# A mixture of experts behind differential attention: rows by number, results in token order

## The chip, the cores and the metric
One NeuronCore of a Trainium2 chip runs the kernel. The metric is the device time of one execution in microseconds, lower is better. The kernel before took 1133.09 us in the median of 3 runs (1131.99 to 1135.56).

## The reference
Input `x` is 4 x 1024 x 256, so 4096 tokens of 256 values, float32. With `xn = layernorm(x)` it computes:

```
q, k  = xn wq^T, xn wk^T          # 8 heads x 2 halves x 32
v     = xn wv^T                   # 8 heads x 32
a     = softmax(q1 k1^T / sqrt(32), causal) - lambda * softmax(q2 k2^T / sqrt(32), causal)
s     = rmsnorm(a v, in groups of 4 values) * (1 - L_INIT), times wo^T
top 2 of 8 experts per token by xn router^T + bias, weights = softmax of the two logits
f_e   = ((clip(up, 7) + 1) * g * sigmoid(1.702 g)) down_e + bias_e,   g = min(gate, 7)
out   = x + s * silu(w0 * f_e0(xn) + w1 * f_e1(xn))
```

Each expert has a 256 x 512 matrix (gate and up) and a 256 x 256 matrix (down).

## The kernel before
It has four blocks that run one after another. At the end of each all engines meet before the next begins.

**Block 1, layer norm, projections, routing.** A loop over 8 chunks of 512 tokens. VectorE normalises, TensorE turns the rows and multiplies by the weights, with each operand split into a high and a low part. ScalarE (`high_parts`) and VectorE (`low_parts`) move the products to four `PARTS` buffers, which SyncE stores to DRAM (L306 to L313); ScalarE waits for the store before it uses a buffer again. Per chunk SyncE also stores 1152 KB of zeros to `xs_dram` (L303), so that places that no token fills are defined, and stores the normalised rows to `xn_dram`. VectorE ranks the experts of each token (`rank`). After the last chunk it turns the choices into slots (L488 to L539). Each expert gets whole tiles of 128 slots, 72 tiles in all. A token's slot is the first slot of its expert plus the number of tokens before it. For that VectorE makes prefix sums over 32 token tiles (five doublings, L497 and L498) and adds the rank inside the tile (L528 to L534).

**Block 2, attention.** 16 iterations of two heads, each of 8 frames (`p` 0 to 7) that pair a long and a short query tile. TensorE scores and turns probabilities, VectorE takes maxima and combines the two softmaxes, ScalarE exponentiates and copies out. GpSimd copies V (`copy_v`, L795), moves each frame's output from `Ob` to `VO` (`keep_rows`, L808), and keeps the sums (`keep_d1`, L833). It also sorts the tokens: per iteration it loads two tiles of `xn_dram` (L814), copies their slots (L815), and issues four indirect DMAs (L826), each of which scatters 128 rows of 1 KB to their slots in `xs_dram`. SyncE loads Q and K one iteration ahead, and an expert's weights and biases in each of the iterations 0 to 7.

**Block 3, experts.** 72 tiles, two sets of buffers (`u` 0 and 1), in 36 loop iterations. SyncE loads a tile of `xs_dram` as soon as TensorE has turned the one two tiles earlier (`xs_turned`, L1166). TensorE works in the order gate and up of tile n+1, turning tile n+2, down of tile n-1, turning the activation of tile n. VectorE runs `activate` (n), `hidden` and `gate` (n+1), `output` (n-1, L1381). ScalarE stores the output from its own queue (`store`, L1312) to `ys_dram`, in slot order. GpSimd does nothing here.

**Block 4, join.** 8 chunks of 512 tokens. GpSimd copies the chunk's slots and weights (L1482, L1483) to fixed tiles and gathers each token's two result rows from `ys_dram`:

```
pool.wait_ge(picked, credited(b, 4, 2 * h + 1))
pool.sem_inc(gather_begun, 1)
for i in range(CT):
    for k in range(TOP_K):
        pool.indirect_dma_start(yg[h][:, i, k, :], None, ys_dram, ...yslot[h][:, i, k:k + 1]...)
```

That is 8 indirect DMAs per chunk. ScalarE scales the first expert's rows (L1562), VectorE adds the second's (L1635), normalises the attention output (L1622 to L1654), and gates and adds (L1660 to L1670). TensorE turns and projects in between. SyncE loads `x` and stores the result.

Of the kernel before, what the change touches and what calls it, by code (L numbers as in the profile page):

```python
# [6 lines left out]
F32 = mybir.dt.float32  # L7
# [60 lines left out]
LONG0, SHORT, LONG1 = 0, 1, 2  # L68
UNITS = 3 * NP
# [31 lines left out]
SORT_AT = {1: (0, 0), 2: (0, 1), 3: (1, 0), 4: (1, 1)}  # L101
# [10 lines left out]
def build(nc, x, wqk, wv, wo, lam, rw, rb, gu, gub, dn, dnb, out):  # L112
    with ExitStack() as ctx:
# [11 lines left out]
        xs_dram = nc.dram_tensor("xs_dram", (SLOT_TILES * P, D), F32, kind="Internal").ap()  # L125
        ys_dram = nc.dram_tensor("ys_dram", (SLOT_TILES * P, D), F32, kind="Internal").ap()
# [19 lines left out]
        slot_of = sb("slot_of", [P, T // P, TOP_K], U32)  # L146

# [16 lines left out]

        consts_done = sem("consts_done")
# [5 lines left out]
        with ExitStack() as ph:  # L171
# [3 lines left out]
            zeros = sb("zeros", [P, SLOT_TILES // NCH * D], where=ph)  # L175
            before = sb("before", [P, E, E], where=ph)
# [3 lines left out]
            count_f = sb("count_f", [P, SLOT_TILES], where=ph)  # L180
            count_128 = sb("count_128", [P, T // P], where=ph)
            logits = sb("logits", [P, T // P, E], where=ph)
            cmp = sb("cmp", [P, T // P * E * TOP_K + 2 * SLOT_TILES * E], where=ph)
            ranks = sb("ranks", [P, 3, QT, E], where=ph)
            chosen = sb("chosen", [P, TOP_K, T // P, E], where=ph)
            chosen_b = sb("chosen_b", [P, T // P, E], BF16, where=ph)
            top = sb("top", [P, 6, T // P], where=ph)
            run = [sb(f"run{i}", [P, T // P, E], where=ph) for i in range(2)]
            per_e = sb("per_e", [P, 8, E], where=ph)
# [36 lines left out]
            zeros_ready = sem("zeros_ready")  # L226
            zeros_stored = sem("zeros_stored")
# [14 lines left out]
            with nc.Block() as block:  # L242
                @block.gpsimd
                def _(pool):
# [19 lines left out]
                    nc.gpsimd.memset(zeros[:], 0.0).then_inc(zeros_ready, 1)  # L264

                    nc.gpsimd.memset(before[:], 1.0).then_inc(const_step, 1)
# [5 lines left out]
                    nc.gpsimd.affine_select(out=before[:], in_=before[:], compare_op=ALU.is_gt, fill=0.0, base=0,  # L272
# [6 lines left out]
                    nc.gpsimd.tensor_copy(count_f[:], count_i[:]).then_inc(const_step, 1)  # L279
                    pool.wait_ge(const_step, 16)  # L280
                    nc.gpsimd.tensor_scalar(count_128[:], count_f[:, 0:T // P], float(P), None, ALU.mult
# [3 lines left out]
                def _(sp):  # L285
# [13 lines left out]
                    sp.wait_ge(zeros_ready, 1)  # L299
                    xs_v = xs_dram.rearrange("(n p r) d -> n p (r d)", p=P, r=SLOT_TILES // NCH)  # L300
# [30 lines left out]
                    sp.wait_ge(zeros_stored, 16 * NCH)  # L331

                @block.vector
                def _(dve):
# [58 lines left out]
                    def rank(b):  # L393
# [16 lines left out]
                        then(nc.vector.tensor_tensor(c3, c3, before[:].rearrange("p e f -> p (e f)").unsqueeze(1)  # L410
# [65 lines left out]

                    steps = [0]
# [7 lines left out]
                    NT = T // P  # L485
                    ck = cmp[:, 0:TOP_K * NT * E].rearrange("p (k t e) -> p k t e", k=TOP_K, e=E)

                    nc.vector.tensor_tensor(top[:, 2], top[:, 1], top[:, 0], ALU.subtract).then_inc(gap_ready, 1)  # L488

                    dve.wait_ge(ranks_bank, 1)  # L490
                    pre = bank6[:, 0:NT * E].rearrange("p (t e) -> p t e", e=E)
                    tot = bank7[:, 0:NT * E].rearrange("p (t e) -> p t e", e=E)
                    nc.vector.memset(run[0][:, 0:1, :], 0.0)
                    then(nc.vector.tensor_copy(run[0][:, 1:NT, :], tot[:, 0:NT - 1, :]))
                    src, span = 0, 1
                    while span < NT:
                        nc.vector.tensor_copy(run[1 - src][:, 0:span, :], run[src][:, 0:span, :])  # L497
# [1210 lines left out]
```

## Time and profile before

| | |
|---|---|
| median of 3 runs | 1133.09 us |
| profiled execution | 1132.22 us |
| its span | 1130.4 us |
| TensorE, VectorE, ScalarE, GpSimd busy | 83%, 83%, 69%, 20% |
| DMA | 178.11 MB, 158 GB/s |
| granted clock of TensorE | 0.945 |

The span is from the first to the last instruction. Busy time counts instructions of an engine, without those that only wait, branch or issue DMAs on SyncE and ScalarE. GpSimd is different: its indirect DMAs are made by the engine itself and count as busy. "Idle before" names what ended an engine's wait. The four blocks lie at about 0 to 182, 182 to 760, 769 to 1013 and 1013.6 to 1130 us.

### The profile page before, as it was taken

What the parts mean: (1) busy time and instruction counts of PE and PEld (TensorE: products, weight loads), DVE (VectorE), ACT (ScalarE), POOL (GpSimd) and SP (SyncE); (2) the same over time, 40 slices, a digit from 0 to 9 for tenths busy, and PEclk for the clock granted to TensorE, in tenths of its full rate; (3) what the DMA queues carried; (4) which work ended last, traced back from release to release, by engine and by line L of the source; (5) the groups of instructions that cost most, each with busy time, mean ns of one, the idle gap of its engine ahead of it and who ended that gap; (6) DMA issues with size and microseconds to landing.
All of it is one profiled execution on the core that took longest, in us unless ns stands there. A gap on an engine that the chain in (4) does not pass through costs nothing. (4 is left out here: it accounts for less than half of the span.)

```text
span 1130.4 us, 25744 instructions
## 1 busy us (share of the span) xinstructions
PE 941.0 (83%) x6626; PEld 657.1 (58%) x6627; DVE 937.8 (83%) x1872; ACT 777.8 (69%) x1982; POOL 225.3 (20%) x427
## 2 busy tenths in 40 slices
PE   5888875989889898998989989876999999962665
PEld 4666653666666666666666666653555555541544
DVE  6676757999999999999999999963777777764887
ACT  3444334999999999999999999972333333325563
POOL 2000000122223222232222322220000000007771
PEclk9999985999999999999999999997999999996677
DMA  7988967578676786766657566501222222223553
GB/s 274 353 318 304 329 256 202 126 179 197 165 178 154 178 194 164 178 156 138 152 120 165 129 140 151 118 20 50 80 79 83 83 80 79 84 82 104 163 179 118
DMA packets 92410, 178.11 MB, mean 158 GB/s; under 512 B 11744, under 2 KB 50144, under 8 KB 91360
## 3 DMA queue, kind: packets, MB, share of 16 engines
q1 hardware_dynamic: 74336, 147.38, 48.6%
q0 software_dynamic: 7680, 20.98, 6.3%
q10 hardware_dynamic: 10368, 9.44, 2.5%
q8 instruction: 11, 0.18, 0.1%
q14 instruction: 15, 0.12, 0.0%
HBM read 108.56 MB, written 69.21 MB: 157 GB/s over the span
## 5 line engine op out<-in xcount | busy, mean ns | idle before, releaser
L1032 DVE TENSOR_REDUCE nmax<-bank 128x1 f32<-128x1024 f32 (+3 forms) x256 | 259.9, 1015 | 4.2 <-PE bank L864 4.1
L965 ACT ACTIVATE Pr_long<-bank,nmax 128x1024 f32<-128x1024 f32 (+3 forms) x256 | 252.2, 985 | 10.9 <-DVE nmax L1032 10.8
L992 ACT COPY AT<-bank 128x512 f32<-128x512 f32 (+3 forms) x384 | 177.2, 494 | 3.8 <-PE bank L903 1.8
L862 PE MATMUL bank<-Ks_first,Qs_first 128*128 128x512 f32 (+3 forms) x384 | 124.2, 413 | 31.0 <-ACT Pr_short L979 19.8
L979 ACT ACTIVATE Pr_short<-bank,nmax 128x128 f32<-128x128 f32 (+3 forms) x256 | 138.4, 541 | 8.9 <-DVE nmax L1050 1.5
L1224 PE MATMUL bank<-gu_sb,xsT 128*128 x288 | 140.1, 610 | 4.7 <-DVE hid L1341 0.5
L903 PE MATMUL bank<-ident,Pr_long 128*128 128x128 f32 x832 | 127.4, 280 | 18.0 <-DVE Pr_long L1082 17.9
L1082 DVE SCALAR_TENSOR_TENSOR Pr_long<-Pr_long,coef 128x1024 f32<-128x1024 f32 (+3 forms) x128 | 137.4, 1074 | 0.0
L862 PE MATMUL bank<-Ks_second,Qs_second 128*128 128x512 f32 (+3 forms) x384 | 119.5, 400 | 19.8 <-ACT Pr_short L979 19.5
L864 PE MATMUL bank<-maskb,identb 128*128 128x128 bf16 x512 | 118.2, 233 | 0.0
L926 PE MATMUL bank<-AT,Vj 128*32 128x128 f32 x2304 | 108.7, 278 | 0.0
L903 PEld LDWEIGHTS bank<-ident,Pr_long 128*128 128x128 f32 x832 | 90.4, 142 | 31.4 <-issue 27.0
L808 POOL COPY VO<-Ob 128x64 f32 (+1 forms) x128 | 30.3, 237 | 386.3 <-ACT Ob L1001 386.0
L645 PE MATMUL bank<-XNT_parts,wqk_parts 128*128 128x512 f32 x384 | 95.1, 406 | 9.7 <-DVE PARTS L432 8.2
L862 PEld LDWEIGHTS bank<-Ks_first,Qs_first 128*128 128x128 f32 x384 | 66.4, 202 | 59.2 <-ACT Pr_short L979 39.3
L862 PEld LDWEIGHTS bank<-Ks_second,Qs_second 128*128 128x128 f32 x384 | 63.5, 193 | 48.6 <-ACT Pr_short L979 40.5
L645 PEld LDWEIGHTS bank<-XNT_parts,wqk_parts 128*128 128x128 f32 x384 | 73.9, 194 | 28.2 <-DVE PARTS L432 9.3
L864 PEld LDWEIGHTS bank<-maskb,identb 128*128 128x128 bf16 x512 | 49.9, 97 | 67.8 <-issue 50.6
L581 ACT ACTIVATE PARTS<-bank 128x512 fp32r<-128x512 f32 x64 | 38.3, 598 | 60.9 <-PE bank L645 30.8
L1050 DVE TENSOR_REDUCE nmax<-bank 128x1 f32<-128x512 f32 (+1 forms) x128 | 79.0, 618 | 1.3 <-PE bank L864 0.7
L926 PEld LDWEIGHTS bank<-AT,Vj 128*32 128x32 f32 x2304 | 74.4, 109 | 8.8 <-issue 0.3
L1250 PE MATMUL bank<-dn_sb,act_T 128*128 x288 | 76.1, 387 | 2.8 <-ACT act_T L1303 2.7
(147 smaller groups left out, 1633.4 us busy)
## 6 DMA issues: line engine op xcount, KB each, us to landing
q_parts<-PARTS SPq DMA_DIRECT2D x32, 512.0 KB, 3.7
k_parts<-PARTS SPq DMA_DIRECT2D x32, 512.0 KB, 3.7
Qs_first<-q_parts SPq DMA_DIRECT2D x64, 256.0 KB
Ks_first<-k_parts SPq DMA_DIRECT2D x64, 256.0 KB
Qs_second<-q_parts SPq DMA_DIRECT2D x64, 256.0 KB, 5.8
Ks_second<-k_parts SPq DMA_DIRECT2D x64, 256.0 KB, 6.8
xs_dram<-zeros SPq DMA_DIRECT2D x8, 1152.0 KB, 7.3
xs<-xs_dram SPq DMA_DIRECT2D x72, 128.0 KB, 2.0
```

Source lines behind the costliest of these rows:

```text
L645: last = nc.tensor.matmul(qkbank[i % 4], wqk_parts[:, w, c, i * P:(i + 1) * P], XNT_parts[:, r, c, :], start=((c, w, r) == products[0]), s ...
L862: nc.tensor.matmul(at[:, c0:c1], Qs[head][:, m, q * P:(q + 1) * P], Ks[head][:, m, c0:c1], start=True, stop=(c1 < N))
L864: return nc.tensor.matmul(at[:, N - P:N], identb[:], maskb[:], start=False, stop=True)
L903: last = nc.tensor.transpose(tb[u % BANKS][:, i * P:(i + 1) * P], probs[:, 0, kb * P:(kb + 1) * P], ident[:])
L926: last = nc.tensor.matmul(ob[DH * g:DH * (g + 1), 0:P], Vj[head][:, kb, :], AT[unit(p, k) % 6][:, i * P:(i + 1) * P], start=first, stop=final,
L965: nc.scalar.activation(long_probs(p)[:, m, 0:N], long_slot[m][:, 0:N], ACT.Exp, bias=nmax[:, 4 * p + m:4 * p + m + 1], scale=1.0, accum_ou ...
L979: nc.scalar.activation(short_probs(p)[:, m, 0:N], short_at(p, m)[:, 0:N], ACT.Exp, bias=nmax[:, 4 * p + 2 + m:4 * p + 3 + m], scale=1.0, a ...
L992: nc.scalar.copy(AT[u % 6][:, 0:w], tb[u % BANKS][:, 0:w]).then_inc(unit_out, 1)
L1032: nc.vector.tensor_reduce(nmax[:, 4 * p + m:4 * p + m + 1], long_slot[m][:, 0:N], AX.X, ALU.max, negate=True).then_inc(long_maxed, 1)
L1050: nc.vector.tensor_reduce(nmax[:, 4 * p + 2 + m:4 * p + 3 + m], short_slot[:, 0:N], AX.X, ALU.max, negate=True).then_inc(short_maxed, 1)
L1082: nc.vector.scalar_tensor_tensor(out=probs[:, 0, 0:N], in0=probs[:, 1, 0:N], scalar=coef[:, 2 * p + 1:2 * p + 2], in1=probs[:, 0, 0:N], op ...
L1224: last = nc.tensor.matmul(hbank[u], xsT[u][:, c, :], gu_sb[:, c, bass.ds(e, 1), :].rearrange("p o n -> p (o n)"), start=(c == 0), stop=(c ...
```

## The change
- **Row numbers, not rows, are sorted.** In block 1 SyncE stores a 36 KB table of default numbers to `ids_dram` once; the stores of zeros go. In attention, iterations 1 to 8, GpSimd scatters one 4-byte number for each token and choice (`k * 4096 + token`) to its slot in `ids_dram`: 8 indirect DMAs per iteration, 64 in all. The row loads (L814) and the scatters of rows go. After iteration 9's loads SyncE reads the whole table back as 128 x 72 words (`slot_rows`). In the last iteration GpSimd works out the token of each slot (`slot_tokens`) and gathers the first tile of rows.
- **Block 3.** GpSimd gathers each tile of rows from `xn_dram` (`rows_in`), and scatters each tile of results to `y_dram` in token order (`results_out`). SyncE's loads and ScalarE's stores go. VectorE's `output` waits for `rows_ready`, which GpSimd signals after it has copied the tile's row numbers.
- **Block 4.** The eight gathers per chunk go; SyncE loads the chunk's two result rows per token with two plain DMAs of 512 KB.
- **Prefix sums** and slot numbers move from VectorE at the end of block 1 to GpSimd in iteration 0 of attention, frames 0 to 4. Their tiles lie in the memory of the biases of experts 2 to 7, whose loads wait for `routed`.
- **All four blocks** are made with `no_gpsimd_drain=True`.

```diff
-                        sp.dma_start(xs_v[b * 2 + h], zeros[:]).then_inc(zeros_stored, 16)
+                    sp.dma_start(ids_dram.rearrange("(q n) o -> q (n o)", n=2 * P), no_rows[:]).then_inc(ids_cleared, 16)
...
+                    nc.vector.tensor_copy(pre, bank6[:, 0:NT * E].rearrange("p (t e) -> p t e", e=E))
+                    nc.vector.tensor_copy(tot, bank7[:, 0:NT * E].rearrange("p (t e) -> p t e", e=E))
...
+                    then(nc.vector.tensor_reduce(tokens, bank7[:, 0:NT * E].rearrange("p (t e) -> p e t", e=E), AX.X,
+                                                 ALU.add))
...
+                    sp.wait_ge(routed, ROUTE_OPS)
...
+                    sp.wait_ge(ids_sorted, 16 * SORT_ITS * NP)
+                    with nc.allow_non_contiguous_dma("one word of each slot"):
+                        sp.dma_start(slot_rows[:], ids_dram.rearrange("(n p) o -> p (n o)", p=P)
+                                     ).then_inc(rows_known, 16)
...
+                    def double(src, span):
+                        nc.gpsimd.tensor_copy(run[1 - src][:, 0:span, :], run[src][:, 0:span, :])
+                        then(nc.gpsimd.tensor_tensor(run[1 - src][:, span:, :], run[src][:, span:, :],
+                                                     run[src][:, 0:NT - span, :], ALU.add))
...
+                        for n in SORT_AT.get(p, ()):
+                            i, k = n // TOP_K, n % TOP_K
+                            pool.indirect_dma_start(ids_dram, bass.IndirectOffsetOnAxis(sort_slot[:, i, k:k + 1], 0),
+                                                    sort_id[:, i, k:k + 1], None).then_inc(ids_sorted, 16)
...
+            with nc.Block(no_gpsimd_drain=True) as block:
+                @block.gpsimd
+                def _(pool):
+                    def rows_in(it, u):
+
+                        pool.wait_ge(xs_turned, seen(it, u - 2))
+                        nc.gpsimd.tensor_copy(xs_token[u][:], slot_tokens[:, bass.ds(2 * it + u, 1)]
+                                              ).then_inc(tokens_ready, 1)
+                        pool.wait_ge(tokens_ready, 2 * (it - 1) + u + 1)
+
+                        pool.sem_inc(gather_begun, 1)
+                        pool.indirect_dma_start(xs[u][:], None, xn_dram, bass.IndirectOffsetOnAxis(xs_token[u][:], 0)
+                                                ).then_inc(xs_loaded[u], 16)
+
+                    def results_out(it, u):
+
+                        if not (isinstance(it, int) and it == 0):
+                            pool.wait_ge(y_stored[u], 16 * it)
+                        nc.gpsimd.tensor_copy(ys_row[u][:], slot_rows[:, bass.ds(2 * it + u, 1)]
+                                              ).then_inc(rows_ready, 1)
+                        pool.wait_ge(rows_ready, 2 * it + u + 1)
+                        pool.wait_ge(y_ready, seen(it, u))
+
+                        pool.sem_inc(gather_begun, 1)
+                        pool.indirect_dma_start(y_dram, bass.IndirectOffsetOnAxis(ys_row[u][:], 0), ys[u][:], None
+                                                ).then_inc(y_stored[u], 16)
...
+                    with pool.Fori(1, NIT3 - 2) as it:
                         for u in range(2):
-                            load(it, u)
+                            rows_in(it + 2, u)
+                            results_out(it, u)
...
-                    nc.vector.wait_ge(y_stored[u], 16 * (it + 1))
+
+                    nc.vector.wait_ge(rows_ready, 2 * it + u + 1)
...
+                    def load_y(b, h):
+                        for k in range(TOP_K):
+                            sp.dma_start(yg[h][:, :, k, :], y_v[k, b, h]).then_inc(y_loaded[h], 16)
```

## Rows read from the trace of the kernel before
**Rows 1.** Busy time by stage: start:end, length, engines (x instructions), clock, DMA share, GB/s
```profile
0.00:182.00 182.00, 134.95 (x578) 106.16 (x579) 120.78 (x344) 73.06 (x141) 6.69 (x27) 0.95 0.86 303
...
182.00:760.40 578.40, 516.53 (x4992) 368.97 (x4992) 559.71 (x960) 558.28 (x1537) 148.15 (x320) 0.98 0.66 151
...
771.00:1012.00 241.00, 231.38 (x864) 137.00 (x864) 173.93 (x432) 83.46 (x216) 0.00 (x0) 0.99 0.24 77
...
1013.60:1130.40 116.80, 58.18 (x192) 44.97 (x192) 83.41 (x136) 63.00 (x88) 70.41 (x80) 0.69 0.46 144
```
**Rows 2.** The chain that ended last, its shares of the span by line, from the page
```profile
POOL yg L1489 5%; DMA yg<-ys_dram,yslot 0%; PE bank L1535 0%; POOL yslot L1482 0%; ACT ff L1562 0%; DVE root L1641 0%; POOLq L1447 0%; DVE ff L1635 0%; DVE ft L1666 0%; ACT L1571 0%; DVE xr L1670 0%; DVE ft L1660 0%; DVE On L1654 0%; POOL yw L1483 0%; ACT root L1571 0%
```
**Rows 3.** Timeline of the expert stage: start us, us, engine, line
```profile
883.08 0.42 DVE L1381 SCALAR_TENSOR_TENSOR ys<-bank,dnb_sb 128x256 f32<-128x256 f32 x1
...
889.56 0.42 DVE L1381 SCALAR_TENSOR_TENSOR ys<-bank,dnb_sb 128x256 f32<-128x256 f32 x1
...
890.15 0.34 ACTq L1312 DMA_DIRECT2D ys_dram<-ys  x1
```
**Rows 4.** Timeline of the last stage: first and last of VectorE's sums
```profile
1029.01 1.72 DVE L1635 SCALAR_TENSOR_TENSOR ff<-yg,yw,ff 128x256 f32<-128x256 f32 x4 [12.15 <-ACT ff L1562]
...
1112.06 1.67 DVE L1635 SCALAR_TENSOR_TENSOR ff<-yg,yw,ff 128x256 f32<-128x256 f32 x4 [1.16 <-ACT ff L1562]
```
**Rows 5.** The list of waits: us in total, times, longest
```profile
ACT ff L1562 <- DMA yg<-ys_dram,yslot: 30.3, 8, 12.2
```
**Rows 6.** Timeline of GpSimd in the last stage
```profile
1025.55 0.19 POOL L1483 COPY yw<-weight 128x8 f32 x1
...
1026.55 0.97 POOL L1489 DMA_INDIRECT yg<-ys_dram,yslot  x1 [0.81 <-POOL yw L1483]
...
1027.83 0.96 POOL L1489 DMA_INDIRECT yg<-ys_dram,yslot  x1 [0.30 <-issue]
```
**Rows 7.** Indirect DMAs by line: duration ns min/median/max, first and last start
```profile
L1489 POOL DMA_INDIRECT yg<-ys_dram,yslot x64: 949/957/1503, 1015.6 to 1107.5; - x64
...
L826 POOL DMA_INDIRECT xs_dram<-rows,row_slot x64: 983/1047/1238, 209.3 to 752.4; - x64
```
**Rows 8.** Timeline of GpSimd in attention
```profile
752.41 0.98 POOL L826 DMA_INDIRECT xs_dram<-rows,row_slot  x1 [0.45 <-issue]
```
**Rows 9.** Timeline at the ends of block 1 and of block 2
```profile
181.20 0.15 DVE L544 TENSOR_SCALAR lam_s<-lam_s 128x1 f32<-128x1 f32 x1
...
182.07 0.34 SPq L162 DMA_DIRECT2D Qs_second<-q_parts  x1
...
760.13 0.24 POOL L808 COPY VO<-Ob 128x64 f32<-128x64 f32 x1 [0.24 <-ACT Ob L1023]
...
768.86 3.30 SPq L1166 DMA_DIRECT2D xs<-xs_dram  x3
...
771.00 1.20 PE L1210 MATMUL bank<-ident,xs 128*128 128x128 f32 x4 [11.31 <-DMA xs<-xs_dram]
```
**Rows 10.** DMA issues: engine, count, KB each, median us to landing
```profile
xs_dram<-zeros SPq DMA_DIRECT2D x8, 1152.0 KB, 7.3
...
xr<-x SPq DMA_DIRECT2D x8, 512.0 KB, 3.5
...
xs_dram<-rows,row_slot POOLq DMA_INDIRECT x64, 3.6
...
yg<-ys_dram,yslot POOLq DMA_INDIRECT x64, 2.8
...
ys_dram<-ys ACTq DMA_DIRECT2D x72, 128.0 KB, 1.7
```
**Rows 11.** The list of waits, TensorE in block 1
```profile
PE bank L631 <- DVE XN L380: 20.4, 7, 10.2
```
**Rows 12.** Sum of busy time over the stretches 168:171 and 177.4:180.2
```profile
sum 5.80, PE 3.00 PEld 2.47 DVE 5.40 ACT 1.00 POOL 0.00; mean PE 1.50 PEld 1.24 DVE 2.70 ACT 0.50 POOL 0.00
```
**Rows 13.** VectorE's ratio in attention: duration ns min/median/max
```profile
L1069 DVE SCALAR_TENSOR_TENSOR coef<-dsum,lam_s,rec x128: 203/215/356, 188.9 to 753.1; 128x2 f32<-128x2 f32 x128
```

More of the change, by code:

```diff
@@ L68 @@
 LONG0, SHORT, LONG1 = 0, 1, 2
+ROUTE_OPS = 14
 UNITS = 3 * NP
@@ L493, in _ @@
[L493 to L497, printed above, removed]
-                        then(nc.vector.tensor_tensor(run[1 - src][:, span:, :], run[src][:, span:, :],
-                                                     run[src][:, 0:NT - span, :], ALU.add))
-                        src, span = 1 - src, 2 * span
+                    tokens, tiles, first, end, first_slot = (per_e[:, i] for i in range(5))
@@ L501, in _ @@
+                    then(nc.vector.tensor_reduce(tokens, bank7[:, 0:NT * E].rearrange("p (t e) -> p e t", e=E), AX.X,
+                                                 ALU.add))
                     low_parts(B - 1, 1, range(QKT // 2, QKT // 2 + 2))
-                    tokens, tiles, first, end, first_slot = (per_e[:, i] for i in range(5))
-                    then(nc.vector.tensor_tensor(tokens, run[src][:, NT - 1, :], tot[:, NT - 1, :], ALU.add))
-                    ce = cmp[:, 0:E * NT].rearrange("p (e t) -> p e t", e=E)
+                    ce = rcmp[:, 0:E * NT].rearrange("p (e t) -> p e t", e=E)
@@ L699, in build @@
             nmax = sb("nmax", [P, 2 * NQ], where=ph)
-            rows = [sb(f"rows{u}", [P, D], where=ph) for u in range(2)]
-            row_slot = [sb(f"row_slot{u}", [P, TOP_K], U32, where=ph) for u in range(2)]
+            sort_slot = sb("sort_slot", [P, NP // 2, TOP_K], U32, where=ph)
+            sort_id = sb("sort_id", [P, NP // 2, TOP_K], I32, where=ph)
             rec = sb("rec", [P, NQ], where=ph)
@@ L1120, in build @@
         with ExitStack() as ph:
-            xs = [sb(f"xs{u}", [P, D], where=ph) for u in range(2)]
+            xs = [xs_first, sb("xs_second", [P, D], where=ph)]
+            xs_token = [sb(f"xs_token{u}", [P, 1], I32, where=ph) for u in range(2)]
+            ys_row = [sb(f"ys_row{u}", [P, 1], I32, where=ph) for u in range(2)]
             xsT = [sb(f"xsT{u}", [P, HC, P], where=ph) for u in range(2)]
@@ L1129, in build @@
             ys = [sb(f"ys{u}", [P, D], where=ph) for u in range(2)]
-            xs_loaded = [sem(f"xs_loaded{u}") for u in range(2)]
+            tokens_ready = sem("tokens_ready")
+            rows_ready = sem("rows_ready")
+            gather_begun = sem("gather_begun")
             xs_turned = sem("xs_turned")
@@ L1404, in build @@
             yg = [sb(f"yg{h}", [P, CT, TOP_K, D], where=ph) for h in range(2)]
-            yslot = [sb(f"yslot{h}", [P, CT, TOP_K], U32, where=ph) for h in range(2)]
             yw = [sb(f"yw{h}", [P, CT, TOP_K], where=ph) for h in range(2)]
```

285 lines of the change are left out of this document (169 added, 116 removed).

## The prediction
> **What bounds the kernel now.** I read the totals by stage first, because the program has four blocks that follow one another. The first stage (0 to 182 us: layer norm, Q/K/V and router products) keeps the DMA engines 86% busy and TensorE 135 of 182 us. Attention (182 to 760) is VectorE's: 560 of 578 us. The expert stage (771 to 1012) is TensorE's: 231 of 241 us, with GpSimd at zero. The last stage (1014 to 1130) has GpSimd at 70 us, and the chain that ended last, read next, has GpSimd's gathers (L1489) as its longest line [rows 1, 2]. Then the distances inside the stages. Two outputs of one buffer, `ys`, lie 889.56 - 883.08 = 6.48 us apart, so an expert tile takes 3.24 us [rows 3]. The last stage's chunks go by GpSimd: the second halves of the expert sums (L1635) first start at 1029.01 and last at 1112.06, 83.05 / 7 = 11.86 us per chunk, and by the list of waits ScalarE waited 30.3 us for gathered rows [rows 4, 5]. The change takes transfers away from SyncE and ScalarE in the expert stage and gives them to GpSimd, so the price of one GpSimd transfer decides.
>
> **That price.** In the last stage the kernel already does what the new expert loop does: copy an index to a fixed place, wait for that copy, add to a semaphore, start the indirect DMA. The last copy before the DMA takes 0.19 us; from its end (1025.74) to the DMA's start (1026.55) are 0.81 us; the next DMA follows 0.30 after the end of the one before [rows 6]. The median gather is 0.957 us long on GpSimd, the median scatter 1.047 [rows 7]: I use 0.96 and 1.05. Where nothing waits for the copy's own completion, as in attention, the gap between copy and DMA is still 0.45 us [rows 8].
>
> **The expert stage, step by step.** For each of 72 tiles GpSimd now runs `rows_in` and `results_out`.
> - `rows_in`: copy 0.19, gap 0.81, gather 0.96: 1.96 us. Its wait on `xs_turned` is met in steady state, for TensorE has over a microsecond to spare by then.
> - `results_out`: copy 0.19. VectorE's output now waits for `rows_ready`, that is for this copy, and GpSimd then waits for that output: about 0.06 to reach VectorE (an estimate from the 0.17 us by which a store on ScalarE's queue follows an output, 889.98 to 890.15 [rows 3]), 0.42 for the output, 0.10 back; then 0.70 to the DMA's start (the 0.81 less 0.11 for the copy's own signal), and the scatter 1.05: 2.52 us.
> Together 4.48, taken as 4.45 us per tile. Behind GpSimd's wait for an output stand the next gather and its copy; behind VectorE's wait stand the next tile's activation and bias, 173.93 / 72 = 2.42 us of VectorE per tile with the output itself [rows 1], which fit into the rest. So GpSimd becomes the bound: 72 x (4.45 - 3.24) = +87.1 us. Below, without VectorE in the loop, 2 x (0.19 + 0.81) + 0.96 + 1.05 = 4.01, or +55. Above, with four hold-ups of 0.15 us by VectorE, 5.05, or +130 (a rival below). I stay near the row that has the whole sequence.
>
> **The edges of that stage.** Attention's last work ends at 760.37 (GpSimd's copy), and the next block's first DMA goes at 768.86: 8.5 us in which nothing runs. After the first block the same exit takes 182.07 - 181.35 = 0.72 us, and no GpSimd DMA was before it [rows 9]. I put the difference, 7.8 us, down to the drain that is dropped: -7.8 (bounds 0 and -8.5). The first rows are then there already, but the second gather is issued only inside the block, and TensorE turns tile 1 before tile 0's first product: 0.7 + 2.8 us to landing [rows 10] against 771.00 - 768.86 = 2.14 now: +1.4. At the end a scatter (0.7, then 2.8 to 3.6 to land) takes the place of a store (0.17 + 1.7): +2.
>
> **The last stage.** Eight gathers per chunk become two plain loads, so GpSimd leaves. Late next is VectorE, with 83.41 / 8 = 10.43 us busy per chunk [rows 1]; with 0.4 of small gaps 10.8: 7 x (11.86 - 10.8) = -7.4. The first chunk waited 12.2 us for its rows [rows 5]; two loads of 512 KB, at 3.5 us for the one of `x` [rows 10], should land in 5.5, and 1.7 of ScalarE follow: VectorE starts its sum some 7.2 us after the block begins (about 1013.6, where its stretch is cut [rows 1]), not 15.4: -8. Bounds for both together: 0 (loads that are late by as much as the gathers) and -18. I take -15.4. The last block's drain had the last chunk's 20 us as cover, so dropping it gives nothing.
>
> **The first stage.** Eight stores of 1152 KB of zeros go, each 7.3 us to landing [rows 10], in a stage whose stores ScalarE waits for. Of this only what reaches TensorE counts: its waits for the normalised rows, 20.4 us less the 10.2 of the start [rows 11]. I take half, -5 (bounds 0 and -10). The routing arithmetic: the prefix sums (168 to 171 us) and the slot numbers (177.4 to 180.2), together 5.40 us of VectorE, leave it [rows 12]; two copies from PSUM and a wider sum, 3 x 0.42, come. That would be -4.1, but the stores of the last parts end the stage almost as late: -3 (bounds 0 and -5).
>
> **Attention.** GpSimd gets 14 counted steps in iteration 0. No GpSimd addition is in the trace. The same work took VectorE 5.40 us [rows 12]; between that and three times as long on GpSimd, the lot is 5 to 16 us over five frames of 578 / 128 = 4.5 us, in most of which GpSimd waits for `Ob`; `o_kept` has a slack of two frames. Its reads can hold up VectorE: the 128x2 ratio, 0.20 us at best, was once 0.356 [rows 13]. The 32 row loads and 30-odd copies go, which gives some back. Sum +1 (bounds -3 and +6). The 64 scatters are as many as before, now two in some frames: 0.24 + 0.45 + 2 x 1.05 + 0.30 = 3.1 us, under a frame.
> The slot table comes back as 128 x 72 single words. A 1 KB piece costs 0.24 x 16 x 241 / (72 x 256) = 0.050 us of a DMA engine in the expert stage [rows 1]. 9,216 of them at that price are 29 us on 16 engines. They start when the loads for iteration 10 are out, and the loads behind them are wanted a full iteration of 36 us later less their own 6: covered, by a hair. I take 0, bounds 0 and +30.
> The Trainium skill, "DMA: Bandwidth & Descriptors", Rules for kernel authors, says that a non-contiguous last dim becomes one descriptor per element. No row here shows such a transfer; were the table instead read in 128 pieces, the sum would be the same 0, and only the upper bound would go.
>
> **Sum.** 1132.2 (the profiled execution) - 5 - 3 + 1 - 7.8 + 1.4 + 87.1 + 2 - 15.4 = 1192.5. The median of the runs is 0.9 above the profiled one: 1193.
>
> **Rivals.**
> - GpSimd keeps up. If its sequencer runs ahead of both waits, a tile costs 2 x (0.19 + 0.45) + 0.96 + 1.05 = 3.29 us, TensorE stays the bound and all the gains remain: 1132.2 - 26.8 + 72 x 0.05 + 0.9 = 1110, faster. It decides at 3.24 + 26 / 72 = 3.6 us per tile. For it: consecutive DMAs are only 0.30 apart [rows 6]. Against it: the 0.81 us stand before each of the eight groups, and the output's wait cannot be passed. Chance 0.10, and 0.04 for something between, near 1133 to 1150.
> - VectorE locks GpSimd out. Attention shows a hold-up the other way, 0.356 against 0.203 us for the same ratio, 0.15 [rows 13]. If each of GpSimd's four instructions per tile meets one: 72 x 0.6 = +43, 1236. For it: the old indirect DMAs reach 1.50 us at most against a median of 0.957 [rows 7]. Against it: that median is near the minimum of 0.949. Chance 0.08. The Trainium skill, "SBUF — State Buffer", Who interferes with whom, has the rule: a VectorE operation in a two-port mode and GpSimd lock each other out for the whole instruction. It names a GpSimd DMA of 620 ns that became 3100 ns; nothing in this trace is so long.
> - The table read is dear: pieces at twice the price make 58 us, some 30 of them TensorE's wait in iteration 11: 1223. Chance 0.05.
> - The change doesn't do what it says: the 8.5 us are no drain and stay. 1201. Chance 0.04.
> - The forecast: 0.69.
>
> **How the numbers follow.** 1193 is the likeliest. Of its own terms the tile's price weighs most: 4.01 and fuller gains give 1150, 5.05 gives 1236. The range 1140 to 1238 leaves out the keep-up case, part of the middle, and the worst of the lock. A change under 0.3% (3.4 us, about what can be measured) has 0.02; faster 0.11; slower 0.87.
>
> **What would show it.** In the expert stage: GpSimd busy above 170 of some 320 us, outputs 4.4 us apart per tile, TensorE waiting for `ys` or `xs`, and VectorE's outputs waiting for a GpSimd copy of `ys_row`. Under 1 us between attention's last copy and the next block. In the last stage chunks 10.8 us apart and no GpSimd on the chain. A shorter wait of ScalarE for part stores. Wrong if an expert tile stays under 3.6 us, if the DMA follows its index copy within 0.5 us, or if attention has one gap of tens of microseconds near iteration 11.

## The result, and the profile after

The changed kernel takes 1307.5 us (median of 4 runs, 1307.35 to 1308.3) against 1134.0 for the kernel before on the same chip: a ratio of 1.153, 95% interval 1.151 to 1.154. The forecast was 1193, range 1140 to 1238. Slower was right, and the expert stage is slower in the way that was worked out; but attention, for which I had put 1 us, lost 96.

The stages after, with the same columns as [rows 1]; the cuts follow the new boundaries:

```profile
0.00:178.00 178.00, 138.33 (x578) 108.67 (x579) 115.06 (x328) 72.92 (x141) 5.29 (x28) 0.95 0.76 257
178.00:850.00 672.00, 538.01 (x4971) 383.34 (x4971) 562.37 (x960) 562.08 (x1535) 127.72 (x293) 0.91 0.64 111
856.00:1197.00 341.00, 251.24 (x852) 132.72 (x852) 167.05 (x427) 78.32 (x213) 174.98 (x278) 0.98 0.17 53
1198.00:1305.80 107.80, 56.59 (x202) 43.68 (x200) 84.45 (x139) 62.78 (x89) 4.69 (x13) 0.74 0.49 159
```

Attention has the same work on VectorE as before (562 us busy, 560 in [rows 1]), but spread over 672 us and not 578: waits were added, not work. In the expert stage TensorE's share of the time fell from 231 of 241 us to 251 of 341, and GpSimd went from 0 to 175. The last row begins 8 us before the last block does (1206.00), so it holds the end of the expert stage too. In the last stage GpSimd is gone and VectorE is what is left.

I cut both executions at the same four events and set the differences beside the forecast. All times in us.

| stretch | before | after | difference | forecast |
|---|---|---|---|---|
| start to attention | 182.07 | 178.05 | -4.0 | -8 |
| attention, to its last copy on GpSimd | 578.3 | 674.6 | +96.3 | +1 |
| last copy to the first gate product | 11.9 | 4.3 | -7.7 | -6.4 |
| first gate product to the last `ys` | 239.1 | 345.4 | +106.3 | +87.1 |
| last `ys` to the last block | 2.2 | 3.7 | +1.5 | +2 |
| last block to the end | 116.8 | 99.8 | -17.0 | -15.4 |
| sum (spans 1130.4 and 1305.8) | | | +175.4 | +60.3 |

Where attention's time went stands in the list of waits (us in total, times, longest):

```profile
DVE ys L1490 <- POOL ys_row L1267: 141.8, 69, 4.8
POOL y_dram L1273 <- DVE ys L1490: 101.5, 70, 3.5
...
DVE nmax L1138 <- PE bank L952: 78.2, 10, 12.9
...
POOL d_all L914 <- DMA ids_dram<-sort_id,sort_slot: 73.2, 8, 12.3
...
PE bank L997 <- POOL Vj L811: 68.1, 8, 11.7
```

Read from below: TensorE waited 8 times, 8.5 us each, for the copy of V (`Vj`, L811); GpSimd stood 8 times before the copy that precedes it (`d_all`, L914), 9.2 us each, until scatters of row numbers had landed; VectorE in turn stood for scores, 78.2 us in all. Eight is the number of iterations that sort. It is one wait, `pool.wait_ge(ids_sorted, ...)` at the end of each of these iterations. GpSimd's timeline shows it (start, length, then in brackets the idle time before and what ended it):

```profile
313.95 0.98 POOL L895 DMA_INDIRECT ids_dram<-sort_id,sort_slot  x1 [0.43 <-issue]
317.33 0.24 POOL L824 COPY VO<-Ob 128x64 f32 x1 [2.40 <-ACT Ob L1089]
326.59 0.19 POOL L914 COPY d_all<-dsum 128x8 f32 x1 [9.02 <-DMA ids_dram<-sort_id,sort_slot]
327.05 0.73 POOL L811 COPY Vj<-VO 128x256 f32 x2 [0.28 <-issue]
```

The last scatter of this iteration started at 313.95, and the wait for all eight ended 12.6 us later; a row scatter of before took 3.6 to land [rows 10]. And the scatters were not alone in being late: the expert weights that SyncE loads in the same iterations took 16.6 us to land, 9.4 before:

```profile
gu_sb<-gu SPq DMA_DIRECT2D x8, 512.0 KB, 16.6
```

The 16.6 us are not a constant: in e3 and e7 below, which have the same attention, it was 12.2 and 12.8.

An iteration with scatters lasts 44.8 to 49.3 us by the starts of its first copy of V, one from iteration 10 on 35.0 to 35.4, about as all do before. The rest of the 96 us are a pause of 6.5 us at 257.5, in which ScalarE, VectorE and TensorE stop together and SyncE issues no load (256.89 to 263.67), and a lower TensorE clock after each stall (granted clock .91 over the stage, .98 before [rows 1]; .50, that is 1.2 of 2.4 GHz, in the 4 us after the wait shown).

The expert tile, on GpSimd:

```profile
1000.09 0.20 POOL L1255 COPY xs_token<-slot_tokens 128x1 int32 x1
1001.11 1.00 POOL L1260 DMA_INDIRECT xs_first<-xn_dram,xs_token  x1 [0.81 <-POOL xs_token L1255]
1002.11 0.20 POOL L1267 COPY ys_row<-slot_rows 128x1 int32 x1
1003.71 1.18 POOL L1273 DMA_INDIRECT y_dram<-ys,ys_row  x1 [1.41 <-DVE ys L1490]
1004.89 0.20 POOL L1255 COPY xs_token<-slot_tokens 128x1 int32 x1
```

From copy to copy are 4.80 us, without a gap that GpSimd could use. Over two tiles VectorE's outputs start at 1002.44 and 1011.95, 4.755 us a tile, 3.24 before [rows 3]; over 140 us in the middle of the stage the mean is 4.8.

In the last stage VectorE's first sum starts 7.3 us after the block does (15.4 before [rows 4]), and the chunks follow 10.80 us apart, from 1213.28 to 1288.86 (11.86 before), without GpSimd.

### The profile page after: what moved, and what is told of

Its sections match the earlier page's. It is cut to its first block and busy times, and to the rows that moved or that the text cites. A ratio compares the mean times of both kernels' runs of the same rounds, so it can differ in the third digit from the quotient of the medians.

```text
span 1305.8 us, 25730 instructions
## 1 busy us (share of the span) xinstructions
PE 986.5 (76%) x6626; PEld 670.1 (51%) x6627; DVE 929.7 (71%) x1856; ACT 777.5 (60%) x1982; POOL 315.6 (24%) x618
## 5 line engine op out<-in xcount | busy, mean ns | idle before, releaser
L1120 DVE TENSOR_REDUCE nmax<-bank 128x1 f32<-128x1024 f32 (+3 forms) x256 | 260.1, 1016 | 21.2 <-PE bank L952 14.5
L1402 ACT COPY xsT<-bank 128x256 f32<-128x256 f32 x72 | 26.8, 372 | 222.7 <-PE bank L1331 222.7
L950 PE MATMUL bank<-Ks_first,Qs_first 128*128 128x512 f32 (+3 forms) x384 | 128.1, 424 | 34.8 <-ACT Pr_short L1067 25.1
L991 PE MATMUL bank<-ident,Pr_long 128*128 128x128 f32 x832 | 131.6, 287 | 18.0 <-DVE Pr_long L1170 17.0
L950 PE MATMUL bank<-Ks_second,Qs_second 128*128 128x512 f32 (+3 forms) x384 | 124.8, 414 | 18.3 <-ACT Pr_short L1067 18.2
L1138 DVE TENSOR_REDUCE nmax<-bank 128x1 f32<-128x512 f32 (+1 forms) x128 | 79.2, 618 | 78.9 <-PE bank L952 78.2
L1490 DVE SCALAR_TENSOR_TENSOR ys<-bank,dnb_sb 128x256 f32<-128x256 f32 x72 | 30.6, 424 | 142.3 <-POOL ys_row L1267 141.8
L1014 PE MATMUL bank<-AT,Vj 128*32 128x128 f32 x2304 | 114.2, 288 | 0.0
L991 PEld LDWEIGHTS bank<-ident,Pr_long 128*128 128x128 f32 x832 | 94.8, 147 | 31.2 <-issue 26.5
L1273 POOL DMA_INDIRECT y_dram<-ys,ys_row x72 | 80.8, 1122 | 108.6 <-DVE ys L1490 101.5
L997 PE MATMUL bank<-sum_strips,Ob 128*128 128x64 f32 x256 | 46.0, 263 | 68.7 <-POOL Vj L811 68.1
L950 PEld LDWEIGHTS bank<-Ks_second,Qs_second 128*128 128x128 f32 x384 | 66.8, 203 | 45.2 <-ACT Pr_short L1067 36.8
```

Of the source, the lines that this page charges most:

```text
L950: nc.tensor.matmul(at[:, c0:c1], Qs[head][:, m, q * P:(q + 1) * P], Ks[head][:, m, c0:c1], start=True, stop=(c1 < N))
L991: last = nc.tensor.transpose(tb[u % BANKS][:, i * P:(i + 1) * P], probs[:, 0, kb * P:(kb + 1) * P], ident[:])
L1014: last = nc.tensor.matmul(ob[DH * g:DH * (g + 1), 0:P], Vj[head][:, kb, :], AT[unit(p, k) % 6][:, i * P:(i + 1) * P], start=first, stop=final,
L1120: nc.vector.tensor_reduce(nmax[:, 4 * p + m:4 * p + m + 1], long_slot[m][:, 0:N], AX.X, ALU.max, negate=True).then_inc(long_maxed, 1)
L1273: pool.indirect_dma_start(y_dram, bass.IndirectOffsetOnAxis(ys_row[u][:], 0), ys[u][:], None).then_inc(y_stored[u], 16)
```

## The experiments

Twelve kernels ran, each timed against the kernel before on the same chip. "Attention" is from the first copy of V to the end of the last copy of output rows, "experts" from the first gate product to the last `ys`, both of the profiled execution; "iterations" are the lengths of iterations 1 to 8 by the starts of their first copy of V.

| kernel | us, median | ratio to before, 95% | attention | iterations | experts |
|---|---|---|---|---|---|
| before | 1134.0 | | 578.0 | 35.3 to 36.0 | 239.1 |
| after | 1307.5 | 1.151 to 1.154 | 674.3 | 44.8 to 49.3 | 345.4 |
| e1, wait behind the copies | 1248.7 | 1.099 to 1.103 | 608.2 | 36.1 to 40.5 | 345.8 |
| e2, 1 KB rows | 1234.0 | 1.082 to 1.092 | 605.0 | 37.3 to 39.7 | 344.5 |
| e3, numbers before the gather | 1253.9 | 1.100 to 1.108 | 664.6 | 43.8 to 47.5 | 303.5 |
| e4, before without drain | 1126.1 | .990 to .993 | 578.5 | 35.4 to 36.2 | 236.9 |
| e5, early scatters | 1266.8 | 1.112 to 1.116 | 631.7 | 37.8 to 43.7 | 345.5 |
| e6, 64-byte rows | 1226.5 | 1.076 to 1.080 | 596.2 | 35.5 to 39.7 | 344.1 |
| e7, no index copies | 1219.8 | 1.071 to 1.077 | 658.5 | 43.8 to 47.0 | 269.7 |
| e8, e5 and e7 | 1187.4 | 1.042 to 1.046 | 631.4 | 37.3 to 44.7 | 269.6 |
| e9, e1, e7 and 64-byte table | 1142.9 | 1.005 to 1.011 | 581.2 | 35.4 to 35.9 | 270.0 |
| e10, number in the row | 1120.4 | .985 to .990 | 580.0 | 35.4 to 36.2 | 244.2 |
| e11, 32-byte rows | 1221.7 | 1.074 to 1.081 | 589.4 | 34.9 to 38.7 | 343.4 |
| e12, words 64 bytes apart | 1225.5 | 1.078 to 1.082 | 588.8 | 34.9 to 38.9 | 345.9 |

### The wait in attention

**e1** moves the wait.

```
                         if p == 0:
+                            if not isinstance(it, int):
+                                pool.wait_ge(ids_sorted, 16 * NP * (it - 1))
                             tiles = bass.ds((it - 1) * (NP // 2), NP // 2)
...
-                        if p == NP - 1:
-                            pool.wait_ge(ids_sorted, 16 * NP * it)
```

> The changed kernel with one wait moved: GpSimd's wait for the eight id scatters of an attention iteration stands at the start of the next iteration's sorting, behind the two copies of V and the first copy of output rows, instead of at the end of its own iteration. Same scatters, same places. Theory A (the 96 us that attention lost are this wait holding up the copies of V that the matmuls need): the eight waits (73 us) and the clock dips behind them (about 12) go, attention from 674.6 to about 590 us, the kernel from 1307.5 to about 1222. Theory B (the scatters themselves slow the other transfers, and the matmuls would be late for their Q and K in any case): attention stays above 650, the kernel above 1285. In between (the wait is still not over where it now stands, and the copy of output rows behind it is late): 1235 to 1270.

Attention lost 66 of its 96 extra us, and the kernel came to 1248.7, between the two theories and in the middle band. (The execution profiled was the fastest of five, 8 us under the median, so 66 is at the upper end; by the medians the whole kernel gained 59.) The wait was a cause, but not the whole: an iteration stayed at about 39 us. In its list of waits over attention, part is the moved wait, and part is TensorE waiting for K, which the kernel before does not do in these iterations:

```profile
POOL sort_slot L889 <- DMA ids_dram<-sort_id,sort_slot: 19.2, 6, 4.5
...
PE bank L951 <- DMA Ks_first<-k_parts: 5.4, 3, 3.0
```

**e2** leaves the wait and changes the bytes.

```
-   pool.indirect_dma_start(ids_dram, bass.IndirectOffsetOnAxis(sort_slot[:, i, k:k + 1], 0),
-                           sort_id[:, i, k:k + 1], None).then_inc(ids_sorted, 16)
+   pool.indirect_dma_start(wide_dram, bass.IndirectOffsetOnAxis(sort_slot[:, i, k:k + 1], 0),
+                           wo_sb[:, 0, 0:D], None).then_inc(ids_sorted, 16)
```

> The changed kernel with the wait where it is, but each of the 64 scatters writes 1 KB to its slot's row of another table (a slice of the output weights as payload) instead of 4 bytes to the slot table; so the results reach no token, and the last stage reads normalised rows in their place, in the same sizes. Theory A2 (words of 4 bytes are slow to land, rows of 1 KB are not: 3.6 us in the kernel before): the last scatter has landed by the time of the wait, attention about 590 us, the kernel about 1222. Theory C (the size doesn't matter, the scatters are late because they stand behind the 1.15 MB of expert weights that are issued in the same frames): waits of 5 us or more stay in iterations with weights, 256 times the bytes make them longer if anything, attention 660 to 700, the kernel 1290 to 1335.

The row numbers don't reach their table here, nor in e6 and e11, but the expert stage does the same work in the same time (343.4 to 344.5 us, 345.4 after). 256 times the bytes, and the wait at the same place fell from 73.2 us to 8.7; the weights landed in 9.6 us again:

```profile
POOL d_all L915 <- DMA wide_dram<-wo_sb,sort_slot: 8.7, 4, 3.1
...
gu_sb<-gu SPq DMA_DIRECT2D x8, 512.0 KB, 9.6
```

Theory C (scatters late because they stand behind the weights) falls: the same weights, in the same frames, no longer delay anything. It is the other way round, the scatters of words delayed the weights.

**e5** is e1 with `SORT_AT = {1: (0, 1), 2: (2, 3), 3: (4, 5), 4: (6, 7)}`.

> The kernel of the wait behind the copies, and the eight scatters of an iteration issued in pairs in its frames 1 to 4, not spread to frame 6, so that they have four frames more to land before the wait. In that kernel an iteration with scatters took 39 us, 35.4 without. Theory A (only waits are left: 19 us in all where the wait now stands): the wait is gone, 37 us or less an iteration, attention 580 to 595 us, the kernel 1220 to 1235. Theory B2 (the scatters of words hold the DMA engines, so the next K is late for the matmuls, 3.0 us in one iteration read, wherever they are issued): still 38 to 41 us an iteration, the kernel within 10 us of 1248.

It was 18 us slower than e1, which neither theory had. The wait is gone from the list, yet iterations take up to 43.7 us: the pairs fall on SyncE's loads of Q and K, and the pauses in which several engines stop at once, 6.5 us in the changed kernel, now add up on VectorE to 32 us ("remote" is what the profile calls a releaser that it doesn't find):

```profile
DVE nmax L1133 <- remote: 15.4, 5, 4.3
...
DVE nmax L1121 <- remote: 12.2, 4, 5.6
...
DVE nmax L1139 <- remote: 4.8, 1, 4.8
```

Giving the scatters more time does not help where what they hold up is everything else. So the wait is not the whole of the loss: with the wait moved, e1 still lost 30 us in attention, and e5, whose list has no wait for scatters at all, 54.

**e6** and **e11** are e2 with `wo_sb[:, 0, 0:16]` and `wo_sb[:, 0, 0:8]` and a table of that width.

> The kernel whose scatters write 1 KB, with 64 bytes in their place (16 words; wait at the end of the iteration, as changed; results reach no token and the last stage reads normalised rows). With 1 KB it took 1234 us and the expert weights landed in 9.6 us, with 4 bytes 1307.5 and 16.6. Theory A3 (any write below some size is slow): 64 bytes are as slow as 4, an iteration of 45 to 48 us, the kernel 1290 to 1315, weights 15 us or more. Theory A4 (only the single word is slow): 1225 to 1245, weights about 9.6 us.

> The kernel whose scatters write 1 KB or 64 bytes, with 32 bytes (wait at the end of the iteration; results reach no token, the last stage reads normalised rows). 64 bytes gave 1226 us and weights in 9.8 us, 4 bytes 1307.5 and 16.6. If only a single word is slow: 1220 to 1245 and 10 us. If any write of less than 64 bytes is slow: 1290 to 1315 and 15 us or more.

Both fast (weights 9.8 and 9.7 us). So no size limit at 64 or 32 bytes; either the single word is special, or the table in which the words lie side by side.

**e12** tells these apart. It keeps the word and spaces the slots.

```
-        ids_dram = nc.dram_tensor("ids_dram", (SLOT_TILES * P, 1), I32, kind="Internal").ap()
+        ids_dram = nc.dram_tensor("ids_dram", (SLOT_TILES * P * ID_WORDS, 1), I32, kind="Internal").ap()
...
+                            pool.sem_inc(scatter_begun, 1)
+                            nc.gpsimd.tensor_scalar(sort_slot[:], sort_slot[:], ID_WORDS, None, ALU.mult
+                                                    ).then_inc(slots_known, 1)
+                            pool.wait_ge(slots_known, it)
                             pool.sem_inc(scatter_begun, 1)
```

> The changed kernel with its scatters still of one word of 4 bytes, but each slot's word at the start of 64 bytes of its own (the slot numbers are multiplied by 16 on GpSimd, one more small instruction an iteration; the cleared table is 16 times as large). Nothing else is moved, all is computed. Writes of 32, 64 and 1024 bytes in such rows gave 1222 to 1234 us. If a write of one word is slow by itself: 1290 to 1315 as changed, weights landing in 15 us or more. If it was many words written side by side into the same memory line: 1220 to 1240, weights in about 10 us.

1225.5 us, weights 9.7, attention 85 us shorter than after. A word of 4 bytes is not slow to write by itself; the same words written 4 bytes apart into a table of 36 KB are. Of the 10.8 us that attention still lacks in e12, the wait at the end of the iterations (11.6 us in 7 waits) could account for all. The two kernels have a stretch that lines up to some hundredths of a microsecond: a scatter, then SyncE's loads of Q and K. After (350 to 354), then e12 (331 to 335); the last two numbers are the DMA engines' share and GB/s:

```profile
350.00:352.00 2.00, 1.77 (x17) 1.37 (x20) 2.00 (x6) 2.00 (x6) 1.46 (x2) 1.00 1.21 31
352.00:354.00 2.00, 2.00 (x26) 1.35 (x27) 2.00 (x3) 2.00 (x8) 0.47 (x1) 1.00 1.02 53
```

```profile
331.00:333.00 2.00, 1.77 (x17) 1.38 (x20) 2.00 (x6) 2.00 (x6) 1.45 (x2) 1.00 0.97 236
333.00:335.00 2.00, 2.00 (x26) 1.35 (x27) 2.00 (x3) 2.00 (x8) 0.49 (x1) 1.00 1.06 203
```

The engines do the same work in both. The DMA engines are full in both, but move 31 and 53 GB/s beside scatters into the dense table, 236 and 203 beside the same scatters into a spaced one. A full DMA share at an eighth to a quarter of the usual GB/s is the mark to look for.

### The expert tile

**e3** puts the copy of the results' row numbers ahead of the gather:

```
+                            row_numbers(it, u)
                             rows_in(it + 2, u)
                             results_out(it, u)
```

> The changed kernel with GpSimd's copy of the row numbers for the results (and the release of VectorE's output with it) put ahead of the gather of the tile after next, not behind it; the same instructions, in another order. Theory D (a tile's 4.75 us is one chain on GpSimd: copy .20, gap .81, gather 1.00, copy .20, wait for VectorE 1.41, scatter 1.15, and the 1.41 is VectorE answering a copy that comes too late): gather and scatter follow each other, a tile costs 3.4 to 3.7 us, the stage loses 70 to 95 us, the kernel about 1225. Theory E (the transfers or VectorE's own work of 3.24 us in 4.75 set the time): a tile stays above 4.4 us, the kernel above 1280.

The stage lost 42 us, half of what theory D gave it, and a tile takes 4.2 us. VectorE's wait for the copy went from 141.8 us to 7.0, so that part is shown. Late next is TensorE, for the gathered rows (waits over 860 to 1140):

```profile
DVE ys L1495 <- PE bank L1376: 62.6, 60, 3.4
PEld bank L1336 <- DMA xs_second<-xn_dram,xs_token: 59.6, 33, 4.1
```

Theory D saw GpSimd's own chain alone. With two buffers the rows of tile t+2 can be asked for only when tile t is turned, and GpSimd stood 59.1 us before its scatters in these 280 us. The profile names no releaser for that; that it was the output is my reading of the program.

**e7** keeps e3's order and writes the loop out, so that no index is copied:

```
-                        nc.gpsimd.tensor_copy(xs_token[u][:], slot_tokens[:, bass.ds(2 * it + u, 1)]
-                                              ).then_inc(tokens_ready, 1)
-                        pool.wait_ge(tokens_ready, 2 * (it - 1) + u + 1)
...
-                    with pool.Fori(1, NIT3 - 2) as it:
+                    for it in range(1, NIT3 - 2):
```

> The changed kernel with GpSimd's loop over the tiles written out, so that gathers and scatters take their row numbers from the slot table directly: 142 index copies and the waits on them go, and VectorE's output waits for the stores alone, a count raised ahead of the gather. With the row numbers ahead of the gather a tile took 4.2 us. Theory H (two tiles are one loop through two buffers: down product, VectorE's output, scatter 1.1, index copies and gap 1.2, gather 1.0, landing, turn, next down product: 8.2 us then): without the copies 6.6 to 7.2 us for two tiles, 3.3 to 3.6 a tile, the stage 238 to 262 us, the kernel 1207 to 1228. Theory I (with all transfers of the stage on GpSimd's queue, descriptors or bandwidth set 4 us a tile): the stage above 290 us, the kernel above 1250.

269.7 us for the stage, just above theory H's upper end and far from theory I's 290: 34 us less than in e3, gone with the copies and with the loop itself, which this run does not separate. What is left is an uneven pair, 3.0 and 4.2 us, in which GpSimd's scatter waits in turn for the store before it and for VectorE:

```profile
1004.80 1.18 POOL L1270 DMA_INDIRECT y_dram<-ys,slot_rows  x1 [1.92 <-DVE ys L1491]
1006.28 0.97 POOL L1256 DMA_INDIRECT xs_second<-xn_dram,slot_tokens  x1 [0.30 <-issue]
1007.80 1.09 POOL L1270 DMA_INDIRECT y_dram<-ys,slot_rows  x1 [0.55 <-DMA y_dram<-ys,slot_rows]
```

Whether a third buffer would close it wasn't tried.

**e8** has e5's scatters and e7's experts.

> The changed kernel with both repairs together: scatters early with their wait behind the copies of V, and no index copies in the expert stage. If the two losses are separate: the sum of what each gives alone, 178 + about 590 + 4 + about 250 + 104, so 1120 to 1135, as fast as the kernel before or a little faster. If attention keeps 39 us an iteration and the experts 3.6 us a tile: 1145 to 1155.

1187.4. The two are nearly separate (1307.5 - 40.7 - 87.7 = 1179.1 would be the sum), but the guess for attention was made before e5 was known to be the worse place, and fell with it.

### The drain, and two versions of the whole

**e4** is the kernel before with `nc.Block(no_gpsimd_drain=True)` four times.

> The kernel before with the one part alone that leaves out GpSimd's drain at the end of all four blocks. Theory F (as forecast: 7.8 us go between attention and the experts, the other block ends have GpSimd idle long before): 1124 to 1128, 0.5 to 0.9 per cent faster. Theory G (the wait at the barrier was for something else that stays): 1131 to 1135.

As in theory F. From the last copy of attention (763.55 to 763.79) to the first gate product (767.7) are 3.9 us, 11.9 before: the 8 us were the drain.

**e9** takes the changed kernel, the wait of e1, the loop of e7 and a table of 64-byte rows whose first word is the number.

```
                             pool.indirect_dma_start(ids_dram, bass.IndirectOffsetOnAxis(sort_slot[:, i, k:k + 1], 0),
-                                                    sort_id[:, i, k:k + 1], None).then_inc(ids_sorted, 16)
+                                                    sort_id[:, n:n + ID_WORDS], None).then_inc(ids_sorted, 16)
```

> The changed kernel repaired in three places, all of it still computed: the slot table has rows of 64 bytes, of which the first word is the row number (each scatter writes 16 words, the number and whatever stands behind it), the wait stands behind the copies of V, and the experts' gathers and scatters take their numbers without copies. If the word-sized writes were all that attention lost beyond the wait: 36 to 37 us an iteration with scatters as with 64-byte rows before, attention 585 to 598, experts 270 as without copies, the kernel 1135 to 1150. If the table of 64-byte rows costs elsewhere (0.6 MB of cleared rows in the first stage, the read of one word in 64 bytes): up to 15 us more.

1142.9: attention is back at 581.2 and 35.4 to 35.9 us an iteration, so wait and table together are all but 3 us of what it had lost. What still separates the kernel from the one before is the experts' 270 us.

**e10** is the kernel before with the number of a result's row carried behind the row itself (GpSimd sorts rows of 264 words, 256 of them data, and SyncE loads them so), no drain, and the last stage of the changed kernel.

```
+                        sp.wait_ge(ids_taken, seen(it, u - 2))
                         sp.dma_start(xs[u][:], xs_v[it, u]).then_inc(xs_loaded[u], 16)
...
+                    def take(t):
+                        pool.wait_ge(xs_loaded[t % 2], 16 * (t // 2 + 1))
+                        nc.gpsimd.tensor_copy(slot_rows[:, t:t + 1], xs[t % 2][:, D:D + 1].bitcast(I32)
+                                              ).then_inc(ids_taken, 1)
...
+                        pool.indirect_dma_start(y_dram, bass.IndirectOffsetOnAxis(slot_rows[:, t:t + 1], 0),
+                                                ys[t % 2][:], None).then_inc(y_stored[t % 2], 16)
```

> The kernel before, with its sorted rows kept and each row number carried in its row: a row sorted by GpSimd is 264 words, 256 of data and the number of its result, so the experts' load by SyncE brings both, and GpSimd only scatters the results to token order; the last stage is that of the changed kernel, and no block drains GpSimd. GpSimd then has one copy of .2 and one scatter of 1.15 us a tile, under the 3.24 us of VectorE. Theory D (it was the load of GpSimd, not the scatter as such): experts 235 to 250 us, attention within 5 us of 578, last stage 17 less than before, drain 8 less: 1105 to 1125, faster than before by 1 to 2.5 per cent. Rival (the scatter's longer way from VectorE through GpSimd to memory and back binds the two output buffers): experts 260 to 285 us, the kernel 1130 to 1160.

1120.4 us, 1.0 to 1.5% faster than before and the fastest of all. The experts with 264-word loads and one scatter a tile, then the last stage:

```profile
768.00:1012.00 244.00, 236.74 (x860) 134.13 (x860) 172.84 (x432) 77.74 (x215) 91.14 (x141) 0.99 0.25 77
1014.00:1117.80 103.80, 54.85 (x192) 42.57 (x192) 83.32 (x136) 62.41 (x88) 1.48 (x8) 0.75 0.49 163
```

GpSimd is busy 91 of 244 us, not 175 of 341, and TensorE is the bound again. But most of the 14.5 us gained are not the scatter's: leaving out the drain alone gave 9.4 (e4). The last block takes 101.9 us for 116.8, the experts 244.2 for 239.1, and the first stage and attention some 3.5 more. What is left for results in token order is about 5 us, and the intervals of e4 (.990 to .993) and e10 (.985 to .990) only just part. So it pays a little, as long as a tile costs GpSimd one indirect transfer.

## Why the prediction was wrong

**The step that failed** is in "Attention": "The 64 scatters are as many as before, now two in some frames: 0.24 + 0.45 + 2 x 1.05 + 0.30 = 3.1 us, under a frame", within the sum +1 (bounds -3 and +6). It counted what a scatter costs its engine, and that was right: 954 to 1882 ns, median 978, against 1.05 us. It left out the landing, and what the scatters do to other transfers, and so two things that the experiments price. The kernel before waits at the end of an iteration for scatters issued in frames 1 to 4, the changed one for scatters up to frame 6, and in both the next copies of V stand behind that wait (e1 takes back 66 us of 96 by moving it). And the words of the new table lie side by side; beside them the DMA engines were full at an eighth to a quarter of the GB/s (e12 takes back 85 us by spacing them). The two overlap, 66 and 85 of 96: a late landing costs most where a wait shows it. But they are not the same, since without the wait 30 us (e1) and 54 us (e5) stayed; e9, with the wait moved and the entries apart, is within 3.2 us of the kernel before. What I did work out on small transfers was the read of the table, 9,216 words; it landed in 13.7 us and nobody waited for it. I priced the reads of words and forgot the writes. Had attention kept its +1, the kernel would have come to about 1212, inside the range.

The Trainium skill, "DMA: Bandwidth & Descriptors", Specifications, has a transfer of less than 512 B done by read-modify-write. By that rule alone one would expect the 64-byte, 32-byte and spaced 4-byte writes of e6, e11 and e12 all to be dear. What could be measured, the weights beside them, was not late (9.8, 9.7 and 9.7 us, 9.6 beside 1 KB rows); only neighbours in a dense table made it so. The rule as stated does not tell these cases apart.

**A term mis-sized:** the expert tile, 4.45 us in the forecast, measured 4.755. 72 x (4.755 - 3.24) = +109, and the stage shows +106.3 for +87.1. `rows_in` was 2.01 us for 1.96; `results_out` .20 + 1.41 + 1.12 to 1.18 = 2.73 to 2.79 for 2.52: VectorE's answer took 1.41 us where 1.28 stood (of which .06, .10 and the .11 taken off the gap were estimates), and the scatter of 1 KB results 1.12 us in the mean for 1.05. The mechanism is as predicted (GpSimd the bound, VectorE waiting for `ys_row`), and e3 and e7 show both halves of it.

**Right in size:** the drain (-7.7 with the second gather, forecast -6.4; e4 -8), the exit (+1.5 for +2), the last stage (-17.0 for -15.4, its first sum 7.3 us into the block for 7.2). **Half right:** the first stage, -4.0 for -8. Kernels with the same first stage started attention between 175.9 and 179.2 us, against 182.4 and 185.3 for the two without the change, so single executions differ by some 3 us here, and I can't split the term further; ScalarE's wait for part stores only fell from 29.8 to 25.7 us.

**The rivals.** GpSimd did not keep up: the gap after an index copy is .81 us as in [rows 6], never .45. VectorE did not lock it out, but it may have held up the scatters a little. The 70 gathers took between 977 and 998 ns; they settle nothing, for VectorE nearly always stood idle during them, waiting for `ys_row`. In e7 and e9 nearly all gathers do fall on work of VectorE, and they took .94 to .98 us. The Trainium skill, "SBUF — State Buffer", Who interferes with whom, has such a lock for VectorE's two-port modes; nothing of it shows in those gathers. The scatters of results differ: beside VectorE's work most took 1.08 to 1.11 or 1.18 to 1.20 us, as in the lines of the tile above, and the four that met none .98 to 1.00, as the last:

```profile
1203.11 0.98 POOL L1273 DMA_INDIRECT y_dram<-ys,ys_row  x1 [1.44 <-DVE ys L1490]
```

In the mean that is .07 us a tile over the 1.05 that I had used, 5 us for 72 tiles, where the rival had 43. That VectorE is the cause is not shown. The table read was not dear. The drain was one. Of the signs that I named, "one gap of tens of microseconds near iteration 11" looked for the right kind of loss in the wrong place: GpSimd had eight gaps of 4.1 to 12.3 us in iterations 1 to 8.

**What stays open.** The pauses without a known releaser (6.5 us after, some 32 us on VectorE in e5) occur in every kernel with words side by side, are at most .4 us in e2 and e6, and are absent in e4, e9 to e12 and before. That they come with the dense writes is shown, what the engines wait for is not. Why dense words are slow is open too: e12 moved them apart and made the table 16 times as large in one step, so entries that share a stretch of memory and a table that is simply small are not told apart, and no spacing between 4 and 64 bytes was tried for single words.

## What to carry to other kernels

Price a transfer three times: on the engine that issues it, until it lands, and by what it does to the other transfers; then look what stands behind each wait for a landing, for a wait that cost nothing with 3.6 us can cost 9 us with twelve. Before a table of small entries is filled by scattered writes, give each entry its own 64 bytes (32 were enough where the write filled them, e11). And where a tile is already close to its bound, one indirect transfer with its index at hand is affordable (5 us more for 72 tiles in e10), two with their indices at hand cost 31 us (e7) and two with index copies 106: let the data that is loaded anyway carry the index.

## What the runs showed of the hardware

- 64 scatters of 128 words into a dense table: with a wait for them at its end, each iteration with 8 of them cost 9 to 14 us more, and weights landed in 11.6 to 16.6 us (e8, e5, e3, e7, after) for 9.4. Beside the same words 64 bytes apart: 9.7. Beside writes of 32, 64 and 1024 bytes: 9.7, 9.8, 9.6.
- The DMA packets of those word writes hardly show in the DMA share of a stretch without other loads (.01 to .02 right after two of them, at 343 to 348 us of the changed kernel); they show in the share of others' packets, 1.21 at 31 GB/s.
- Reading 9,216 single words took 13.4 to 13.7 us to land, whether they lay side by side or 64 bytes apart.
- An indirect DMA costs GpSimd .95 to 1.0 us as a gather and 1.1 as a scatter of 128 rows of 1 KB (.98 to 1.2), whether its index was copied or taken from a wide table; a copy that it waits for adds .20 and a gap of .81, where .30 lie between DMA and DMA.
